# A gated stack of attention and feed-forward layers on one core: x loaded and stored by pairs of tiles, and the head of the program reordered

## The reference, cut to what matters

```
x = x + tanh(g_xattn[0]) * attention0(layernorm(x), ctx, mask)
x = x + tanh(g_ffn[0])   * ffn0(layernorm(x))
x = x + tanh(g_xattn[1]) * attention1(layernorm(x), ctx)
x = x + tanh(g_ffn[1])   * top-2 mixture of 16 experts + shared expert
x = x + tanh(g_xattn[2]) * attention2(layernorm(x), ctx)
x = x + tanh(g_ffn[2])   * top-1 mixture of 32 experts
x = x + tanh(g_xattn[3]) * slot attention, 3 rounds with a GRU
x = x + tanh(g_ffn[3])   * quantised matmul (int8 range) of layernorm(x)
```

## Time and profile before

| | us |
|---|---|
| median of 3 runs | 342.53 |
| the profiled execution's own time | 342.59 |
| its span | 340.3 |
| PE busy | 313.1 (92%) |
| DVE busy | 223.9 (66%) |
| ACT busy | 132.9 (39%) |
| POOL busy | 57.1 (17%) |

### The profile page before, as it was taken

The page is one execution under the profiler, slowest core; times in us unless marked ns, Lnnn a source line. Parts: engine busy times, 40 slices in busy tenths (PEclk is TensorE's granted clock), DMA queues, the critical chain, the costliest instruction groups (busy, mean ns, idle before and its releaser), DMA issues.

```text
span 340.3 us, 5504 instructions
## 1 busy us (share of the span) xinstructions
PE 313.1 (92%) x2029; PEld 190.5 (56%) x2045; DVE 223.9 (66%) x634; ACT 132.9 (39%) x281; POOL 57.1 (17%) x107
## 2 busy tenths in 40 slices
PE   8889999996898999999999998999999988889993
PEld 4453544762435456774568434578677874766441
DVE  4982842678453776478888393543446658899995
ACT  1344263232546352027212716413243544656200
POOL 7231030344002022021000302020210410111220
PEclk9999999998999999999999999999999999999998
DMA  7960000012000000000000000000000000000002
GB/s 187 328 277 0 2 2 0 0 43 94 2 0 2 0 2 0 0 3 0 0 0 2 3 0 2 0 2 1 2 0 2 0 0 3 0 0 2 0 1 62
DMA packets 6958, 8.70 MB, mean 26 GB/s; under 512 B 3067, under 2 KB 5781, under 8 KB 6677
## 3 DMA queue, kind: packets, MB, share of 16 engines
q1 hardware_dynamic: 6933, 8.37, 7.2%
HBM read 7.84 MB, written 0.52 MB: 25 GB/s over the span
## 4 chain that ended last, share of the span: by engine, by line
PE 64%; DVE 23%; ACT 9%; issue 2%; POOL 1%; DVEq 0%; ACTq 0%
PE psum L846 58%; DVE mx L1537 5%; ACT wide L1232 5%; DVE wide L1700 2%; ACT wide L1343 2%; PE psum L937 2%; DVE xn L1717 1%; DVE wide L1707 1%; DVE wide L1706 1%; DVE xn_t L1716 1%; DVE xn L1410 1%; DVE stats L1401 1%; PE psum L1023 1%; PE psum L975 1%; DVE nmax L1671 1%
## 5 line engine op out<-in xcount | busy, mean ns | idle before, releaser
L1537 DVE TENSOR_REDUCE mx<-psum 128x4 f32<-128x308 f32 x96 | 38.6, 472 | 12.4 <-PE psum L846 12.3
L1232 ACT ACTIVATE wide<-psum 128x512 f32<-128x512 f32 x72 | 36.7, 618 | 13.8 <-PE psum L846 13.5
L846 PE MATMUL psum<-xn_t,w_ffn 128*128 128x512 f32 (+1 forms) x88 | 41.6, 597 | 0.0
L1232 ACT ACTIVATE q<-psum 128x512 f32<-128x512 f32 (+1 forms) x36 | 21.2, 594 | 44.0 <-PE psum L846 38.7
L789 POOL TENSOR_SCALAR nw<-mv 128x2 f32<-128x2 f32 x32 | 7.0, 220 | 169.8 <-DVE mv L1404 169.7
L846 PE MATMUL psum<-halves 128*128 128x512 bf16 x111 | 27.9, 386 | 0.5 <-issue 0.2
L846 PE MATMUL psum<-wide 78*128 78x386 f32 (+1 forms) x69 | 25.2, 505 | 3.3 <-DVE wide L1688 2.1
L846 PE MATMUL psum<-xn_t,early 128*128 128x512 f32 x52 | 26.7, 601 | 0.3
L846 PEld LDWEIGHTS psum<-early,wide 128*128 128x128 f32 x192 | 24.0, 192 | 3.2 <-issue 2.0
L1410 DVE TENSOR_SCALAR xn<-x,mv,nw 128x128 f32<-128x128 f32 x64 | 19.1, 343 | 9.6 <-POOL nw L790 9.4
L846 PEld LDWEIGHTS psum<-w_ffn,wide 128*128 128x128 f32 (+1 forms) x176 | 22.3, 191 | 5.3 <-issue 3.7
(11 more groups left out here) (222 smaller groups left out, 503.7 us busy)
## 6 DMA issues: line engine op xcount, KB each, us to landing
w_ffn<-in_ffn SPq DMA_DIRECT2D x1, 2088.5 KB, 12.6
early<-in_ffn SPq DMA_DIRECT2D x1, 1104.0 KB, 5.0
w_attn<-in_attn SPq DMA_DIRECT2D x1, 640.0 KB, 8.0
w_attn<-in_attn SPq DMA_DIRECT2D x2, 288.0 KB, 6.2
x<-in_x SPq DMA_DIRECT2D x2, 256.0 KB, 3.6
early<-in_ffn SPq DMA_DIRECT2D x1, 512.0 KB, 7.0
out<-x SPq DMA_DIRECT2D x2, 256.0 KB, 2.3
rows<-in_rows SPq DMA_DIRECT2D x1, 468.0 KB, 5.9
```

Of the source, the lines that this page charges most:

```text
L846: return nc.tensor.matmul(out_, lhs, rhs, start=start, stop=stop, **kw)
L1232: A.activation(dst, banks.bank(*name)[0:rows_, 0:cols_], fn, **kw).then_inc(drained["act"], 1)
L1537: last = V.tensor_reduce(mx[:, b, t, lane_heads(g)], banks.bank("max", layer, b, t, g)[:, 0:GK].rearrange("p (h k) -> p h k", k=CTX), AX.X ...
```

## The change

1. x is loaded, for each half, by two transfers of two tiles instead of one of four, with a semaphore each (`x_0_0`, `x_0_1`, ...); `norm` waits for its pair only. `cols` and `ident` go behind `wq0` and `ctx_t`.
2. POOL's memsets of `comb_t` and `nothot_t` move behind its first two `norm` steps.
3. ACT begins with an activation of one column into `table_s`, which nobody reads, so that the table load stands at the program's start.
4. DVE takes `keys_in` ahead of `mask_parts`, and `minus_max` moves from the first to the end of the second.
5. WARM_UP goes from 13 to 9.
6. At the end DVE adds to `x` by two instructions of two tiles each, of which the first waits for the second scaled tile only (`scaled_back`), and SP stores each pair of tiles by a transfer of its own.

```diff
-WARM_UP = 13
+WARM_UP = 9
-    step("keys_in", 0, pe=0.3, act=0.3, dve=1.66, pool=1.7)
-    step("mask_parts", dve=0.9)
+    step("keys_in", 0, pe=0.3, act=0.3, dve=1.6, pool=1.7)
+    step("mask_parts", after=[at("dve", "keys_in", 0)], dve=1.6)
...
             def load_x(b):
-                sp.dma_start(x[:, b, :, :], a["x"][b].rearrange("(t p) d -> p t d", p=P)).then_inc(loaded[f"x_{b}"], 16)
+                for h in range(2):
+                    tiles = slice(2 * h, 2 * h + 2)
+                    sp.dma_start(x[:, b, tiles, :], a["x"][b].rearrange("(t p) d -> p t d", p=P)[:, tiles, :])\
+                      .then_inc(loaded[f"x_{b}_{h}"], 16)
...
             load_x(0)
-            sp.dma_start(cols[:, :], a["cols"]).then_inc(loaded["cols"], 16)
-            sp.dma_start(consts[:, 0:P], a["consts"][:, 0:P]).then_inc(loaded["ident"], 16)
             sp.dma_start(packs["attn0"][:, 0:wq_n], a["attn0"][:, 0:wq_n]).then_inc(loaded["wq0"], 16)
             sp.dma_start(ctx_t[:, :], a["ctx_t"]).then_inc(loaded["ctx_t"], 16)
+            sp.dma_start(consts[:, 0:P], a["consts"][:, 0:P]).then_inc(loaded["ident"], 16)
+            sp.dma_start(cols[:, :], a["cols"]).then_inc(loaded["cols"], 16)
...
-            for b in range(B):
-                sp.wait_ge(x_final[b], 1)
-                sp.dma_start(out[b].rearrange("(t p) d -> p t d", p=P), x[:, b, :, :]).then_inc(stored, 16)
-            sp.wait_ge(stored, 16 * B)
+            for b in (b for phase, b, _ in ORDERS["dve"] if phase == "quantised"):
+                for h in range(2):
+                    tiles = slice(2 * h, 2 * h + 2)
+                    sp.wait_ge(x_final[b], h + 1)
+                    sp.dma_start(out[b].rearrange("(t p) d -> p t d", p=P)[:, tiles, :], x[:, b, tiles, :]).then_inc(stored, 16)
+            sp.wait_ge(stored, 2 * 16 * B)
...
-            G.memset(comb_t[:, :, :].bitcast(F32), 0.0)
-            G.memset(nothot_t[:, :, :], 0.0).then_inc(zeros_made, 1)
             pool.wait_ge(consts_made, 1)
-            for phase, b, args in ORDERS["pool"]:
+            for n, (phase, b, args) in enumerate(ORDERS["pool"]):
                 mine[phase](b, *args)
+                if n == 1:
+                    G.memset(comb_t[:, :, :].bitcast(F32), 0.0)
+                    G.memset(nothot_t[:, :, :], 0.0).then_inc(zeros_made, 1)
...
+            act.wait_ge(idle_made, 1)
+            A.activation(table_s[:, :], idle_t[:, 0:1], ACT.Identity)
...
-                if layer == 0:
-                    V.tensor_scalar(minus_max[:, 0:GK].rearrange("p (h k) -> p h k", h=LH),
-                                    lane_mask[:, :].unsqueeze(2).broadcast_to([P, LH, CTX]), -1.0, None, ALU.mult)\
-                     .then_inc(minus_max_ready, 1)
             def mask_parts(b):
                 dve.wait_ge(loaded["mask"], 16)
                 for i in range(B):
...
+                V.tensor_scalar(minus_max[:, 0:GK].rearrange("p (h k) -> p h k", h=LH),
+                                lane_mask[:, :].unsqueeze(2).broadcast_to([P, LH, CTX]), -1.0, None, ALU.mult)\
+                 .then_inc(minus_max_ready, 1)
...
                 for t in range(T):
                     last = V.scalar_tensor_tensor(xn[:, b, t, :], banks.bank("out", 7, b)[:, t * P:(t + 1) * P],
                                                   route_s[:, b, 3, t:t + 1], rscale_b[:, :], ALU.mult, ALU.mult)
+                    if t == 1:
+                        last.then_inc(scaled_back[b], 1)
                 last.then_inc(drained["dve"], 1)
-                dve.wait_ge(*banks.emptied("out", 7, b))
-                V.scalar_tensor_tensor(flat(x[:, b, :, :]), flat(xn[:, b, :, :]), gain[:, g:g + 1],
-                                       flat(x[:, b, :, :]), ALU.mult, ALU.add).then_inc(x_final[b], 1)
+                for h in range(2):
+                    tiles = slice(2 * h, 2 * h + 2)
+                    if h:
+                        dve.wait_ge(*banks.emptied("out", 7, b))
+                    else:
+                        dve.wait_ge(scaled_back[b], 1)
+                    V.scalar_tensor_tensor(flat(x[:, b, tiles, :]), flat(xn[:, b, tiles, :]), gain[:, g:g + 1],
+                                           flat(x[:, b, tiles, :]), ALU.mult, ALU.add).then_inc(x_final[b], 1)
```

More of the change, by code:

```diff
@@ L592, in program @@
         gain = sb("gain", [P, 8])
+        table_s = sb("table_s", [P, 1])
         gbias = sb("gbias", [P, 4, D])
@@ L669, in program @@
         loaded = {k: sem("loaded_" + k) for k in
-                  ["x_0", "x_1", "ident", "wq0", "ctx_4", "bv", "cols", "rows", "consts", "rounded", "halves", "ctx_t", "ctx_rows", "mask"] + list(PACKS)}
+                  ["x_0_0", "x_0_1", "x_1_0", "x_1_1", "ident", "wq0", "ctx_4", "bv", "cols", "rows", "consts", "rounded", "halves", "ctx_t", "ctx_rows", "mask"] + list(PACKS)}
         filled = sem("bank_filled")
@@ L715, in program @@
         slots_ready = per_half("slots_ready")
+        scaled_back = per_half("scaled_back")
         x_final = per_half("x_final")
@@ L1398, in norm @@
                 if stage == 0:
-                    dve.wait_ge(loaded[f"x_{b}"], 16)
+                    dve.wait_ge(loaded[f"x_{b}_{h}"], 16)
                 for t in tiles:
```

## The result

| | before | after |
|---|---|---|
| median of 20 runs each | 342.55 | 343.06 |
| from, to | 341.79, 343.24 | 342.31, 343.65 |
| profiled execution, its span | 342.59, 340.3 | 343.01, 341.1 |
| PE, DVE, ACT, POOL busy | 313.1, 223.9, 132.9, 57.1 | 313.7, 225.3, 133.3, 57.1 |

What follows compares the result with a forecast made beforehand. The prediction took the head to be bound by DVE's chain with PE arriving within 0.1 us of it. Front +0.15 and back -0.4 gave -0.25 from the median 342.53, so 342.25, no change; range 341.1 to 343.0.

Steps and rivals of the forecast that it cites:

- Front, x and the roots: Head: smaller first load and earlier POOL roots make `xn` whole at 6.4 instead of 7.6, 1.2 us earlier.
- second rival: Head: the moved memsets hold `xn`, front +0.5 to +0.75, total 342.65 to 342.9; chance 0.20.
- Front, DVE: Head: POOL holds the first mask instruction until 9.3; DVE hidden by 1.1 us, reductions at 12.35, front +0.15.
- Front, PE: Head: `query` 0.9 us earlier, but five new fillers (1.08 us) make PE's first scores 0.15 us later.
- The basis: Head: the kernel before starts its first reduction of scores at 12.20, as read from its profile.
- Back: End: sums and stores by pairs, the last store moving 128 KB instead of 256 KB: +0.1 - 0.5 = -0.4 us.
- The first: Head: DVE was the bound, so front gains 0.55 to 1.1 us, total 341.3; chance 0.17.
- The third: End: store time mostly fixed, so no shortening; +0.1 behind, +0.15 in front, total 342.8; chance 0.08.
- The fourth: Middle: the half-clock stretch goes or a second one comes, total 340.7 or 343.8; chance 0.10, half each side.

Runs made afterwards that it cites:

- e2: Changed kernel with the two memsets made to wait until DVE has done minus_max, behind POOL's keys' low part: 341.6, ratio 0.9968.
- e1: Kernel before with only the new end (two sums, two stores per half): 342.36, ratio 0.9994.
- e11: Kernel before with the new end and ten filler matmuls in the middle: 341.46, ratio 0.9977.
- e10: Kernel before with only ten filler matmuls added in the middle: 342.21, ratio 0.9994.
- e8: Changed kernel, memsets and POOL's keys' low part late, no fillers ahead of masks, ten fillers in the middle: 340.16, ratio 0.9935.

## Why the prediction was wrong

- **Front, x and the roots: this step failed.** x at 2.97, the first `xn` at 4.97 and the second pair's start at 5.97 came within 0.2 of it. But "whole at 6.4" was 7.88: the sum has nothing for a hold of `xn` by the two memsets, and it took 1.31 (1.91 instead of 0.60). The prediction had the right mechanism before it as its second rival, with `xn` whole at 7.8 to 8.05, the first reduction at 12.7 to 12.95 and a time of 342.65 to 342.9, and gave it 0.20. What failed is the weighing: "by the row of the root it costs nothing". The root works on 128x2 and the memset on 128x1024, and a row that shows 0.72 us for two columns doesn't show that POOL is on the memory for that long. The row of `minus_max`, an instruction of POOL with hundreds of columns beside one of DVE, was the nearer one, and it was held. e2 shows the cause by its removal: 0.60 again, and the first reduction 1.30 earlier.
- The Trainium skill (SBUF — State Buffer, Who interferes with whom) states for DVE's fast modes that whoever comes first has the shared ports for its whole instruction and the other is blocked. The 1839 ns of one `xn` behind a memset agree, though the hold went on over a second memset. The same section has an instruction of DVE with two SBUF inputs and a reading one of GpSimd contend; 1.22 us for the keys' low part alone and 1.71 beside DVE's `keys_hi` agree with that.
- **Front, DVE.** The first mask instruction was held by the keys' low part as forecast (1.34 us), and DVE was hidden in the end, `q_lo` being done 0.64 before the first reduction. All of it was later, by the hold on `xn`.
- **Front, PE.** The clock rose at about 5.2 rather than at 6.57, so that the fillers ran at 216 ns from 5.37. This gained nothing here, since PE then waited 1.04 for `xn`. It is a second error of the sum, which took the rise to come when it did: without the hold the first reduction is at 11.46 (e2), 0.9 before the 12.35 of the sum. So the 343.06 against 342.25 is what two errors of opposite sign leave, and that the range was missed by only 0.06 is luck. From `query` on each step took what was forecast: `query` to the mask's transposes 11.03 - 8.99 = 2.04 (0.97 + 1.08 = 2.05). That PE and not DVE would bound the head was right; that "PE is no earlier" before held only for an execution with a late rise (e1 has PE's first scores at 10.71, and its reductions follow `q_lo`).
- **The basis.** 12.20 was high: with an early rise the kernel before begins its reductions at 11.76 to 11.96 (e11, e10, e1). Against that the head is 0.8 later, and -0.36 at the end leaves about +0.4, the 0.39 and 0.45 of the table. The sum of the forecast had +0.15 in place of this 0.8, or of the 0.56 that stands between the two profiled executions. An estimate of the whole miss: the first reduction is 0.41 behind the sum's 12.35, and the basis was 0.24 to 0.44 late, 0.65 to 0.85 together; 343.06 is 0.81 over the forecast.
- **Back: right.** -0.4 was forecast; -0.36 is in the trace, and e11 against e10 gives -0.3 to -0.6, by which runs are compared, and e1 -0.40 in the first group of runs and nothing in the second. The last sum ends 1.91 us behind the first scaled tile, 1.92 before, so that all of it is the store's. The profile page's row of the stores went from 2.3 us for 256 KB, from issue to landing, to this:

```profile
out<-x SPq DMA_DIRECT2D x4, 128.0 KB, 1.9
```

- **Rivals.** The first (DVE as the bound, 0.17) fell for the changed kernel, where DVE waits 0.64 for PE; of the kernel before it was right in the three traces whose clock rose early (e1, e10, e11). The second held, at its upper end. The third (no shorter end) fell. The fourth (the clock in the middle) was priced as one event that comes or goes; it is a matter of how many runs have the long stretch, some 0.14 us here. The second and the fourth together give the measured time, within 0.1.

## What to carry to other kernels

When an instruction of POOL with many columns is moved next to a DVE instruction like those held here (`xn`, the mask's copy, `minus_max`: a scalar operation from SBUF to SBUF), count the DVE instruction as held until POOL is done, with the next POOL instruction too if it follows without a gap. Put memsets that nobody needs soon where DVE has no such work; beside `q_lo` and the reductions, which read from PSUM, they cost nothing in e2. Before taking a time from one profiled execution as the basis of a sum, look at when the clock rose in it and what an execution with the other rise would show. Where runs of one kernel spread more than the effect, look for a stretch at half clock behind PE's idle gaps. Fillers in these gaps took 1.06 us off the changed kernel (343.06 to 342.0, ratios 1.0016 and 0.9985), twice what the change itself cost. They are no cure: in the last batch up to 13 of 48 runs still had the stretch, and it then cost more.

## What was not expected of the hardware

- The hold went over two instructions of POOL: DVE's `xn`, started 0.08 us after the first memset, didn't come in between the two, and shows as an instruction of 1839 ns, not as a wait. A hold like this is found in a group's maximum (341/994/1839), not among the releasers.
- The length of the half-rate stretch differs from run to run of the same kernel, 3.4 us (81.7 to 85.1) or 6.8 us (80.3 to 87.1) in the profiled executions, behind the same waits of PE. Between the two groups of runs of the kernel before lie 0.66 us.
- Against the changed kernel, e8 has two more waits on POOL, five fillers fewer in the head and ten more in the middle, and needs 2.9 us less (343.06 to 340.16, each beside its own runs of before), though PE has five matmuls more to do.
